# Two expert layers: ScalarE copies each tile's down weights to a ring, GpSimd copies the row numbers ahead of the scatters

## The reference, cut to what matters

```python
x = x + attention0(layernorm(x), ctx, bias)
x = x + experts0(layernorm(x))      # first expert block
x = x + attention1(layernorm(x), ctx)
x = x + experts1(layernorm(x))      # second expert block

# first expert block, hidden size 256, no biases
h = silu(einsum('td,edh->teh', xf, W1)) * einsum('td,edh->teh', xf, W3)
out = einsum('ted,te->td', einsum('teh,ehd->ted', h, W2), gate)   # gate is zero but for the best 2

# second expert block, hidden size 512, with biases
h = gelu(einsum('td,edp->etp', xf, W1) + b1[:, None, :])
y = einsum('etp,epd->etd', h, W2) + b2[:, None, :]
out = einsum('te,etd->td', router_weights, y)                     # zero but for the best 2
```

## Time and profile before

| | |
|---|---|
| three runs | 545.92, 547.41, 552.12 us; median 547.41 |
| profiled execution | 550.07 us, its span 548.3 us (1.8 us lie around the span) |
| granted TensorE clock, mean | 0.945 |
| first expert stage | first transpose at 194.7 us, last result on DVE at 272.9 us, last scatter starts at 274.95 us |
| values for the second layer | 271.9 to 284.2 us |
| second expert stage | first transpose at 451.1 us, last scatter starts at 530.2 us |
| busy share of the span | PE 86%, DVE 71%, POOL 53%, ACT 40% |

### The profile page before, as it was taken

One profiled execution on the slowest core, in us unless ns is written; L12 is line 12 of the kernel. 1 busy time (PEld: TensorE's weight loads), 2 busy tenths in 40 slices (PEclk: granted clock), 3 DMA queues, 4 the chain that ended last, 5 costly groups with the idle time before them and its releaser, 6 DMA issues.

```text
span 548.3 us, 11636 instructions
## 1 busy us (share of the span) xinstructions
PE 470.7 (86%) x3537; PEld 416.3 (76%) x3537; DVE 389.2 (71%) x1276; ACT 216.7 (40%) x503; POOL 292.9 (53%) x315
## 2 busy tenths in 40 slices
PE   6777998998999878888876999999999779999950
PEld 5556897887887677877763888888889769999950
DVE  4873887888875535445447899999999656767727
ACT  2344665565544423223322534344353314444420
POOL 6235458887764305555623356766766632455540
PEclk9678999999999979899979999999999979999995
DMA  7999950000002922222110000100000012222116
GB/s 211 372 337 358 354 197 11 20 20 20 11 21 78 318 55 69 62 63 62 41 49 28 11 20 31 35 28 22 16 20 11 25 40 68 68 63 72 50 38 208
DMA packets 42930, 49.16 MB, mean 90 GB/s; under 512 B 7809, under 2 KB 28636, under 8 KB 42871
## 3 DMA queue, kind: packets, MB, share of 16 engines
q1 hardware_dynamic: 36991, 39.57, 22.7%
q0 software_dynamic: 4544, 8.44, 4.7%
q10 hardware_dynamic: 1336, 0.43, 0.4%
HBM read 20.97 MB, written 28.35 MB: 90 GB/s over the span
## 4 chain that ended last, share of the span: by engine, by line
PE 59%; POOL 13%; DVE 11%; issue 6%; DMA 3%; ACT 3%; SPq 2%; another core or an unknown queue 2%; POOLq 0%; DVEq 0%; ACTq 0%
PE ps L1590 12%; PE ps L1601 9%; POOL qr L509 5%; PE ps L1551 5%; PE ps L1529 5%; POOL rows L502 4%; PE ps L1506 3%; PE ps L1458 3%; PE ps L1580 3%; PE ps L1543 2%; PE ps L1553 2%; PE ps L1281 2%; PE ps L1631 1%; PE ps L1520 1%
## 5 line engine op out<-in xcount | busy, mean ns | idle before, releaser
L556 POOL DMA_INDIRECT ys<-ysbs,xs x78 | 77.1, 989 | 96.7 <-DVE ysbs L1239 40.8
L1590 PE MATMUL ps<-xsT,wups 128*128 128x128 f32 x624 | 86.6, 284 | 0.2 <-DVE big L1222 0.2
L1590 PEld LDWEIGHTS ps<-xsT,wups 128*128 128x128 f32 x624 | 79.1, 199 | 1.1 <-issue 0.9
L509 POOL TENSOR_TENSOR qr<-qsm,mhalf 128x16 f32<-128x16 f32 x16 | 47.2, 2950 | 22.1 <-DVE qsm L865 22.0
L502 POOL DMA_INDIRECT rows<-pays,slots x32 | 33.4, 1044 | 25.6 <-DVE slots L1000 16.6
L530 POOL DMA_INDIRECT rows<-pays,slots x32 | 32.7, 1022 | 20.3 <-DVE slots L1065 13.4
L521 POOL TENSOR_TENSOR pp<-pp,rden 128x1232 f32<-128x1232 f32 x16 | 36.0, 2251 | 13.4 <-DVE x L1043 10.2
L742 ACT ACTIVATE big<-big 128x512 f32<-128x512 f32 x39 | 24.6, 631 | 44.0 <-issue 17.9
L1601 PE MATMUL ps<-w2b,big 128*128 x312 | 41.1, 275 | 0.0
L1458 PE MATMUL ps<-region_a,pp 128*128 128x90 f32 (+1 forms) x320 | 39.6, 279 | 0.2
L1227 DVE TENSOR_TENSOR big<-ps,b1T 128x512 f32<-128x512 f32 x39 | 27.0, 692 | 17.9 <-PE ps L1590 15.0
(11 more groups left out here) (273 smaller groups left out, 1187.9 us busy)
## 6 DMA issues: line engine op xcount, KB each, us to landing
rows<-empty SPq DMA_DIRECT2D x68, 258.0 KB, 4.0
xs<-rows SPq DMA_DIRECT2D x78, 64.5 KB
region_b<-in_L_ffn_W_dram SPq DMA_DIRECT2D x2, 1024.0 KB, 9.3
region_a<-in_L_ffn_W_dram SPq DMA_DIRECT2D x1, 2048.0 KB
yb_all<-ys SPq DMA_DIRECT2D x16, 128.0 KB, 2.0
keys<-ys SPq DMA_DIRECT2D x8, 256.0 KB
ys<-ysbs,xs POOLq DMA_INDIRECT x78
rows<-pays,slots POOLq DMA_INDIRECT x64
```

Source lines behind the costliest of these rows:

```text
L509: pool.tensor_tensor(qr[s], qsm[s], mhalf[:, 0:H], ALU.pow).then_inc(a["qr"], 1)
L556: pool.indirect_dma_start(ys[l][:, :], bass.IndirectOffsetOnAxis(xs[j % XB][:, D:ROW].bitcast(I32), 0), ysb[j % YB], None, bounds_check=2 ...
L1590: ins = mm(S[s][:, k * P:(k + 1) * P], wup[t % WB][:, k * P:(k + 1) * P], xsT[s], start=True, stop=True)
```

## The change

1. ACT reads each tile's expert number from `sched` and copies the tile's down weights (128 x 256 in the first expert stage, 128 x 512 in the second) to a ring `wdn` of `WD` = 4, which lies in `vals1`. That stands in ACT's round j behind the silu or gelu of tile j-1; the place is free when the down product of tile j-4 is done. PE waits for the copy (`wdn`) before the down product, and reads it at an address fixed in the program. PE loads no register any more.
2. GpSimd copies the row numbers of a tile from `xs` to a small ring `backs` of 12, `AHEAD` = 3 tiles ahead of the scatter, and the scatter takes them from there. SP loads a new tile into `xs` when PE has transposed the old one and GpSimd has copied its row numbers; it no longer waits for the scatter.
3. The result ring grows from `YB` = 4 to 6, so DVE waits for the scatter of six tiles earlier; there are 6 semaphores `sentb` instead of 12.

```diff
-    YB = 4
+    WD = 4
+    YB = 6
+    AHEAD = 3
...
+        wdn = [vals1[:, :, :, :].rearrange("p b c d -> p (b c d)")[:, i * F1:(i + 1) * F1] for i in range(WD)]
...
+        backs = sb("backs", [P, XB], I32)
...
                     if j >= XB:
                         sp.wait_ge(m["Tx"], m.count("Tx", j - XB + 1))
-                        sp.wait_ge(sentb[k], sentb_count(l, j - XB))
+                        sp.wait_ge(m["back"], m.count("back", j - XB + 1))
...
-                for j in range(NJ):
-                    pool.wait_ge(xs_in[j % XB], xs_count(l, j))
-                    pool.wait_ge(m["y"], m.count("y", j + 1))
-                    pool.indirect_dma_start(ys[l][:, :], bass.IndirectOffsetOnAxis(xs[j % XB][:, D:ROW].bitcast(I32), 0),
-                                            ysb[j % YB], None, bounds_check=2 * T - 1,
-                                            oob_is_err=False).then_inc(sentb[j % XB], 16)
+                for i in range(NJ + AHEAD):
+                    j = i
+                    if j < NJ:
+                        pool.wait_ge(xs_in[j % XB], xs_count(l, j))
+                        if j >= XB:
+                            pool.wait_ge(sentb[j % YB], sentb_count(l, j - XB))
+                        pool.tensor_copy(backs[:, j % XB:j % XB + 1], xs[j % XB][:, D:ROW].bitcast(I32)).then_inc(m["back"], 1)
+                    j = i - AHEAD
+                    if 0 <= j < NJ:
+                        pool.wait_ge(m["back"], m.count("back", j + 1))
+                        pool.wait_ge(m["y"], m.count("y", j + 1))
+                        pool.indirect_dma_start(ys[l][:, :], bass.IndirectOffsetOnAxis(backs[:, j % XB:j % XB + 1], 0),
+                                                ysb[j % YB], None, bounds_check=2 * T - 1,
+                                                oob_is_err=False).then_inc(sentb[j % YB], 16)
...
+                    if j < NJ:
+                        e = act.value_load(sched[l][0:1, 0, at(j)], min_val=0, max_val=E - 1)
+                        if j >= WD:
+                            act.wait_ge(m["down"], m.count("down", j - WD + 1))
+                        act.copy(wdn[j % WD][:, 0:nk * D].rearrange("p (k d) -> p k d", d=D), w2[:, e, :, :]).then_inc(m["wdn"], 1)
...
                         if t >= YB:
-                            dve.wait_ge(sentb[(t - YB) % XB], sentb_count(l, t - YB))
+                            dve.wait_ge(sentb[t % YB], sentb_count(l, t - YB))
...
-                        if t + 1 < NJ:
-                            expert.append(pe.value_load(sched[l][0:1, 0, at(t + 1)], min_val=0, max_val=E - 1))
...
                         pe.wait_ge(m["hT"], m.count("hT", t + 1))
+                        pe.wait_ge(m["wdn"], m.count("wdn", t + 1))
                         if t >= 2:
                             pe.wait_ge(m["y"], m.count("y", t - 1))
                         for k in range(nk):
-                            ins = mm((MC, MD)[s][:, 0:D], hT[s][:, k * P:(k + 1) * P], w2[:, expert[t], k, :], start=k == 0, stop=k == nk - 1)
+                            ins = mm((MC, MD)[s][:, 0:D], hT[s][:, k * P:(k + 1) * P], wdn[t % WD][:, k * D:(k + 1) * D], start=k == 0, stop=k == nk - 1)
```

More of the change, by code:

```diff
@@ L274, in bass_xattn_moe_two_layers @@
         ONLY1 = ["c1", "comb", "ffg", "th", "gg", "ffh", "fo", "den", "norm", "scr"]
-        MOE = ["Tx", "xsT", "wup", "up", "act1", "hT", "down", "y"]
+        MOE = ["Tx", "xsT", "wup", "up", "act1", "hT", "down", "y", "back", "wdn"]
         ONCE = {"margin": 1, "cnt": 1, "plan": 9, "sched": 1, "g1": 1, "gates": 3, "zero": 1}
@@ L299, in bass_xattn_moe_two_layers @@
         sent = [sem(f"sent{i}") for i in range(PB)]
-        sentb = [sem(f"sentb{i}") for i in range(XB)]
+        sentb = [sem(f"sentb{i}") for i in range(YB)]
         y_in = [sem(f"y_in{i}") for i in range(4)]
@@ L379, in _ @@
                         sp.wait_ge(m["Tx"], m.count("Tx", j - XB + 1))
-                        sp.wait_ge(sentb[k], sentb_count(l, j - XB))
+                        sp.wait_ge(m["back"], m.count("back", j - XB + 1))
                     r = sp.value_load(sched[l][0:1, 1, at(j)], min_val=0, max_val=SLOTS - P)
                     sp.dma_start(xs[k][:, :], rows[l][bass.ds(r, P), :]).then_inc(xs_in[k], 16)
-                for j in range(NJ - XB, NJ):
-                    sp.wait_ge(sentb[j % XB], sentb_count(l, j))
+                for j in range(NJ - YB, NJ):
+                    sp.wait_ge(sentb[j % YB], sentb_count(l, j))
                 if l == 0:
@@ L723, in moe @@
                     act.copy(b1T[:, :, :], TP[0][:, 0:E * F1 // P].rearrange("p (e k) -> p e k", e=E)).then_inc(pro1["b1Ts"], 1)
+                w2 = w2a if l == 0 else w2b
+                nk = (F0 if l == 0 else F1) // P
+                if l == 0:
+                    act.wait_ge(ld["moe0"], 48)
+                else:
+                    act.wait_ge(ld["moe1"], 64)
+                act.wait_ge(m["sched"], m.count("sched", 1))
                 for j in range(NJ + 1):
@@ L1565, in moe @@
                 m = M[l]
-                w2 = w2a if l == 0 else w2b
                 nk = (F0 if l == 0 else F1) // P
@@ L1572, in moe @@
                     tr(TP[0][:, 0:E * F1 // P], b1rows[:, :], ident[0:E * F1 // P, 0:E * F1 // P]).then_inc(pro1["b1T"], 1)
-                pe.wait_ge(m["sched"], m.count("sched", 1))
-                expert = [pe.value_load(sched[l][0:1, 0, at(0)], min_val=0, max_val=E - 1)]
                 for j in range(NJ + 3):
```

12 lines of the change are left out of this document (6 added, 6 removed).

## The result

| | before | after |
|---|---|---|
| median of 20 runs each, same chip | 548.63 us (544.77 to 552.61) | 551.94 us (548.51 to 557.04) |
| ratio, 95% interval | | 1.0072 (1.0050 to 1.0094) |
| profiled execution | 550.07 us, span 548.3 | 552.54 us, span 550.2 |
| first expert stage, first transpose to end of the last down product | 77.4 us | 80.7 us |
| second expert stage, the same | 77.3 us | 80.4 us |

The change makes the kernel 3.3 us slower, 0.7%. The forecast was 3.6 us faster.

What follows compares the result with a forecast made beforehand. The prediction took PE as the second stage's bound and PE's answers, held up by close scatters, as the first stage's loss. Its terms, -5.0 - 0.5 - 1.0 + 2.3 + 0.6 = -3.6 us, took 547.41 to 543.8 us, range 532 to 556.

Steps and rivals of the forecast that it cites:

- What bounds the kernel now: Second stage: PE; first stage: 15.6 us lost in waits because close GpSimd scatters hold up PE's answers; undisturbed round: DVE full.
- Part 1, PE's addresses: Both expert stages: removing PE's register loads and address arithmetic gains 0; up to 15.6 us if they were the culprit.
- Part 2, ACT's copies: ACT's loads and copies: hidden in first-stage rounds, slower second-stage rounds and starts of both stages, +2.9 us together.
- +0.6 forecast for both starts: Start of each expert stage: ACT's load and a copy stand before the second transposed tile, +0.6 us for both.
- +2.3 forecast: Second-stage rounds: ACT's copy delays the next transposed tile, PE 0.12 us late every two rounds, +2.3 us.
- Part 3, GpSimd: GpSimd's copies between scatters: wider spacing shrinks the waits for PE, -5.0, -0.5 and -1.0 us.
- -5.0, -0.5, -1.0: Gains from shorter waits: first-stage rounds (1.86 to 1.73 us), values behind that stage, long wait of the second stage.
- now 0.97 + 0.30 + 0.22 = 1.49 us: Spacing of queued scatters: busy time, gap and new copy add up, so bursts at 1.27 us become impossible.
- Part 4, rings: SP's earlier loads and DVE's wait for the scatter six tiles back instead of four: 0 for both.
- The sum: All terms, -5.0 - 0.5 - 1.0 + 2.3 + 0.6 = -3.6 us, giving 543.8 us.
- the second rival: First-stage waits stay at 1.86 us a round and ACT's cost is added: +3.4 us, 550.8 us, chance 0.21.
- The last rival: Scatters need a fresh start after GpSimd's copy, 2.00 us apart, GpSimd bounds both stages: +7.2, 554.6 us, chance 0.20.

Runs made afterwards that it cites:

- ring_early: Kernel before plus only ACT's register loads and weight copies, PE at fixed addresses, both placed ahead of the activation; 548.00 us, ratio 1.0048.
- the two kernels in three parts: Kernel before, first stage in thirds: extra GpSimd operation behind scatters in the middle or outer thirds, no SP loads in the last; 552.98 and 554.54 us.
- spaced_4: Kernel before with one further small GpSimd operation behind every scatter; 545.18 us, ratio 0.9957.
- after_again: The changed kernel, unchanged, run again against the kernel before; 552.51 us, ratio 1.0146 (1.0106 by the medians).
- ring_only: Kernel before with only ACT copying the down weights behind the silu or gelu and PE reading fixed addresses; 530.13 us, ratio 1.0059.
- ring_early_2: Kernel before plus ACT's weight copies ahead of the activation, PE at fixed addresses, run a second time; 527.72 us, ratio 0.9990.
- segments_a: Kernel before, first stage: tiles 13 to 25 with an extra GpSimd operation behind each scatter, tiles 26 to 38 without SP loads; 552.98 us.
- backs_only: Kernel before with only GpSimd's row-number copies, SP's loads not waiting for scatters, and 6 result buffers; 526.44 us, ratio 0.9994.
- group B: Kernels run on one chip beside the kernel before, whose median was 546.70 us (23 runs); long waits showed in the first stage.
- plain_store: Kernel before with GpSimd's scatters replaced by SP's plain stores in tile order, rows not going to their tokens' places; 535.26 us, ratio 1.0137.
- no_registers: Kernel before with the schedule written as constants, so no register loads on PE, DVE or SP; 525.29 us, ratio 0.9966.

## Why the prediction was wrong

**What bounds the kernel now.** The reading of the earlier trace rows held in the main: the waits stay when PE loads no register (`after`, `ring_early`), and they go where scatters are spaced (the two kernels in three parts, `spaced_4`). That the scatters do it, and not the quicker round that comes with them, is the likelier reading but not shown. What the prediction lacked is that this is no property of the kernel alone. In three of seven groups the same scatters cost nothing, and the profile of before had no row that could show it. And the earlier trace rows was misread: PE and not DVE bounds the undisturbed round of 1.45 us.

**Part 1, PE's addresses: 0.** Right. The waits stay without PE's register loads (`after_again`, `ring_early`), and where there are no waits the kernel gains 0.3% without all register loads.

**Part 2, ACT's copies: +2.9 us.** Right in size, in part by luck: `ring_only` loses 2.4 us in the second stage and 0.3 in the first. Of the 2.4, 0.7 are there by tile 3 (+0.6 forecast for both starts) and some 1.7 come in the steady rounds (+2.3 forecast). The copy starts 0.65 us behind the gelu's start, not 0.76, and the lateness is not 0.12 us every two rounds but some 0.03 in each, with single rounds that lose 0.2. `ring_early_2` shows the cause: 76.1 us in the second stage with the copy ahead of the gelu.

**Part 3, GpSimd: -6.5 us in all (-5.0, -0.5, -1.0). This is the step that failed**, at "now 0.97 + 0.30 + 0.22 = 1.49 us". The copy takes 0.19 us, but it takes the place of idle time between two scatters: of the 0.30 us 0.16 are left, so the spacing became 1.34 where nothing else held it up. The waits stayed: 13 silus over 1.5 us late in place of 10, the latest 3.47 us against 3.35. And 1.49 would not have helped: in `segments_a` four scatters in a row 1.49 to 1.50 apart stand ahead of waits of 2.9 and 1.9 us. The long wait of the second stage stayed too, 2.95 us of ACT (2.92 in the earlier trace rows), and so did that at the first stage's end (3.29; 3.22 in the earlier trace rows). Where the waits don't show, `backs_only` is at 0.9994 (0.9957 to 1.0031). Part 3 alone was not run where they show; the whole change stands at 1.0146 there in group B, and the ring on ACT without part 3 at 1.0048 and 1.0058 in its two variants, so nothing speaks for a gain by part 3.

**Part 4, rings: 0.** Nothing speaks against it; in `backs_only` it is measured together with part 3.

**The sum.** Without part 3 it was +2.9 us; measured was +3.3. That is the second rival, "nothing else changes", at 550.8 us with a chance of 0.21: its time missed by 1.1 us, its difference of +3.4 by 0.1. So close a hit is luck: the same pair of kernels stood at 1.0072, 1.0146 (1.0106 by the medians) and 1.0021 in three groups.

**The last rival.** GpSimd as the bound by a fresh start behind each copy (0.81 us) didn't come. Of the weight copies of DVE that were to hold up GpSimd's there are rows:

```profile
482.01 0.43 DVE L1232 COPY wups<-region_a 128x512 f32 x1
482.11 0.37 POOL L563 COPY backs<-xs 128x1 int32<-128x1 int32 x1
```

GpSimd's copy ends at 482.48, 0.04 us behind DVE's. In the trace after, 15 of its 78 copies start while DVE copies weights; 14 of them take 273 to 449 ns and end 0.03 to 0.04 us behind DVE's copy, and the 63 others take 183 to 213 ns. So the rule that the Trainium skill gives (SBUF — State Buffer, section Who interferes with whom: a DVE copy of this kind and a GpSimd operation take the shared port in turn) is borne out for these copies. The hold reaches the spacing: in the first stage, the scatters around copies of 0.35 and 0.36 us come 1.48 to 1.49 us apart instead of 1.34. It cost the stage little, since only few copies fall into a weight copy and GpSimd isn't the bound. The prediction was also wrong that the earlier trace rows speak against it for scatters: in the trace before, all 7 scatters over 1.06 us start inside a DVE weight copy, and the longest, 1186 ns, with 0.34 us of it still to run. The floor of about 600 ns that the Trainium skill (DMA: Bandwidth & Descriptors, section Latency and other measured facts) gives a `tensor_load` isn't borne out: ACT's took 272 to 477 ns, median 278.

## What to carry to other kernels

A small operation put between two others of the same engine can hide in the idle time between them, as GpSimd's copy did: look in the timeline at the idle time ahead of each (0.30 us here) before a spacing is built from a sum. When an engine gets more work in a queue on which another waits, ask where in its round it waits anyway and put the work there: the same copies cost 2.4 us behind the gelu and nothing measurable ahead of it. And a wait that the profile can't explain by the program may belong to where and when it ran; time the kernel before in a second group before a forecast rests on its going away.

## What the runs showed of the hardware

- In four groups of seven, long waits for PE (up to 5.59 us of idle ACT) stand behind or among scatters by GpSimd that start 1.27 to 1.5 us apart; most of the late silus start 0.4 to 1.0 us behind the end of the last scatter, some while one still runs. With scatters 1.75 us and more apart, and the round slower with them, none of the long waits came. In the other three groups 38 scatters in a row mostly 1.45 us apart did nothing. The difference is some 20 us, 4% of the kernel. What differs between the groups stays open: nothing in the program does.
- A GpSimd operation that starts while DVE copies 128 x 512 from SBUF to SBUF runs longer. The 128 x 1 copy ends 0.03 to 0.04 us behind DVE's copy. The scatters of 1.09 to 1.16 us in the groups without waits are of this kind: in `backs_only` all 32 scatters over 1.06 us start inside a DVE weight copy, the others take 0.98 at the median. It goes the other way too: DVE's copy takes 0.43 us, and up to 0.71 in the trace before; in `plain_store`, without scatters, none of the 78 takes over 0.43.
- Where DVE isn't in the way, a copy of 128 x 1 on GpSimd between two close scatters costs 0.07 us of spacing for 0.19 us of work.
- The address from a register that the down product reads its weights at costs PE nothing that the second stage shows: 1.896 us a round with it (before) and without any register load (`no_registers`).
